# Rows of 448 bytes in place of 392 in a graph network's second layer, copied out of PSUM by one engine alone

## The reference, cut to what matters

```
def _L1_gnn_ref(features, weight, bias, src, dst, n_nodes):
    deg_out = jnp.maximum(segment_sum(ones_e, src), 1.0)
    deg_in = jnp.maximum(segment_sum(ones_e, dst), 1.0)
    h = features * (deg_out ** (-0.5))[:, None] @ weight
    rst = segment_sum(h[src], dst, num_segments=n_nodes)
    rst = rst * (deg_in ** (-0.5))[:, None] + bias
    return rst
```

## Time and profile before

| | |
|---|---|
| time, median of 3 runs | 9343.21 us (9327.21 to 9349.43) |
| span of the profiled execution | 9400.3 us |
| PE busy | 6254.5 us, 67% of the span |
| DVE busy | 5857.2 us, 62% |
| POOL busy | 5072.2 us, 54% |
| ACT busy | 2528.5 us, 27% |
| DMA queue of SP (q1) | 840.20 MB, 39.7% of 16 engines |
| DMA queue of POOL (q0) | 415.20 MB, 17.5% of 16 engines |

### The profile page before, as it was taken

How to read it: one execution, slowest core, us unless ns; L and a number is a source line. 1 busy time by engine, 2 the same in 40 slices (tenths; PEclk the granted TensorE clock), 3 DMA queues, 4 the chain that set the end, 5 groups by cost and what they waited for, 6 DMA issues and landing times. The chain is left out here.

```text
span 9400.3 us, 184649 instructions
## 1 busy us (share of the span) xinstructions
PE 6254.5 (67%) x34870; PEld 5019.0 (53%) x34871; DVE 5857.2 (62%) x19098; ACT 2528.5 (27%) x8033; POOL 5072.2 (54%) x4975
## 2 busy tenths in 40 slices
PE   1677777777756745546664455566648888888886
PEld 1566666666645533335554222555536666666664
DVE  7566666666649865558887888555554444444444
ACT  5344544545431132211110222000011222212222
POOL 0366666666657400027773000788727777777773
PEclk9555555555555655558886555787775555555556
DMA  7644444444436579998876999545743333333334
GB/s 125 142 138 136 138 138 137 137 139 139 136 95 138 119 126 187 191 190 227 228 222 123 234 252 249 147 140 145 132 102 79 80 82 80 81 80 82 79 82 32
DMA packets 1820627, 1294.74 MB, mean 138 GB/s; under 512 B 1262518, under 2 KB 1641558, under 8 KB 1818560
## 3 DMA queue, kind: packets, MB, share of 16 engines
q1 hardware_dynamic: 1578096, 840.20, 39.7%
q0 software_dynamic: 200704, 415.20, 17.5%
q10 hardware_dynamic: 40912, 29.67, 1.7%
HBM read 922.86 MB, written 361.78 MB: 137 GB/s over the span
## 5 line engine op out<-in xcount | busy, mean ns | idle before, releaser
L1095 POOL DMA_INDIRECT sorted_edges<-arena,idx x1664 | 1623.0, 975 | 951.9 <-issue 632.3
L1894 POOL DMA_INDIRECT arena<-expanded,idx x1152 | 1412.4, 1226 | 1300.8 <-DVE idx L1750 820.4
L2019 POOL DMA_INDIRECT arena<-node_table,idx x1760 | 1660.7, 944 | 557.8 <-issue 389.8
L1010 PE MATMUL banks<-arena,onehot 128*128 x3520 | 1173.1, 441 | 527.3 <-DVE onehot L946 510.6
L1010 PEld LDWEIGHTS banks<-arena,onehot 128*128 128x128 f32 x3520 | 900.6, 318 | 661.8 <-issue 615.4
L1995 PE MATMUL banks<-arena 128*128 128x64 f32 x3520 | 1215.1, 449 | 0.0
L1597 PE MATMUL banks<-arena 128*128 x3520 | 671.0, 361 | 677.2 <-issue 340.5
L1990 PE MATMUL banks<-arena 128*64 128x65 f32 x3520 | 843.7, 343 | 402.3 <-ACT arena L2006 401.4
L1995 PEld LDWEIGHTS banks<-arena 128*128 128x128 f32 x3520 | 884.5, 312 | 211.3
L1836 PE MATMUL banks<-arena 128*128 128x193 bf16 (+1 forms) x4608 | 614.3, 303 | 504.6 <-DVE arena L1802 349.9
L1965 DVE TENSOR_TENSOR arena<-arena,banks 128x64 f32 x1760 | 388.1, 221 | 876.1 <-PE banks L1995 853.8
(11 more groups left out here) (411 smaller groups left out, 11039.8 us busy)
## 6 DMA issues: line engine op xcount, KB each, us to landing
arena<-sorted_edges SPq DMA_DIRECT2D x220, 524.0 KB
arena<-lanes_dram SPq DMA_DIRECT2D x222, 512.0 KB, 13.0
expanded<-arena SPq DMA_DIRECT2D x110, 784.0 KB, 12.8
arena<-in_attr_rows SPq DMA_DIRECT2D x576, 130.0 KB
arena<-sorted_edges SPq DMA_DIRECT2D x110, 536.0 KB
arena<-row_keys SPq DMA_DIRECT2D x110, 512.0 KB
arena<-sorted_edges SPq DMA_DIRECT2D x110, 512.0 KB, 5.7
expanded<-arena SPq DMA_DIRECT2D x110, 512.0 KB
```

The costliest lines, as they stand in the source:

```text
L1010: nc.tensor.matmul(m.psum[j % 4][:, 0:D], m.onehot[:, j % 4, :], m.support[:, bass.ds(blocks[j] * D, D)], start=True, stop=True).then_inc( ...
L1095: nc.gpsimd.indirect_dma_start(m.sorted, bass.IndirectOffsetOnAxis(ap=m.idx[:, j % (4 * CH):j % (4 * CH) + 1], axis=0), m.out_ring[:, slot ...
L1894: nc.gpsimd.indirect_dma_start(to, None, rows, bass.IndirectOffsetOnAxis(ap=m.idx[:, c % aims * groups + g:c % aims * groups + g + 1], axis=0)
L2019: nc.gpsimd.indirect_dma_start(slots[:, j % SLOTS, 0:D], None, m.table, bass.IndirectOffsetOnAxis(ap=m.idx[:, j % SLOTS:j % SLOTS + 1], ax ...
```

## The change

It has three parts, and some tables move.

- `ROW2` goes from 98 to 112 words: a row is 448 bytes, seven times 64, and starts on a border of 64 bytes. The features, the count and the target number stay where they were in the row; the rest is set to zero once. A store grows from 802,816 to 917,504 bytes, a fetch of four rows in the sum by target from 1568 to 1792 bytes a partition.
- ACT copies all four groups out of PSUM. The two semaphores `put_act` and `put_dve` become one, `put`; DVE keeps `take`, and ACT waits for it before it copies groups 1 and 3.
- `reach` compares bf16 numbers (`iota16`) in place of f32.
- `onehot`, `junk`, `marks`, `below` and one of the two attribute one-hots move to another SBUF tensor; their shapes stay.

```
-ROW2 = PARTS // 2 + 2
+ROW2 = 112
+COUNT2 = PARTS // 2
+DST2 = COUNT2 + 1
...
-                    sp.wait_ge(s["put_act"], n * 2 + 2 + 2)
-                    sp.wait_ge(s["put_dve"], n * 2 + 2 + 2)
+                    sp.wait_ge(s["put"], n * 4 + 4 + 4)
...
+                v.memset(out16[:, :, :, PARTS + 4:2 * ROW2].rearrange("p c t f -> p (c t) f"), 0.0).then_inc(s["blank"], 1)
...
-                    v.tensor_scalar(m.reached[0:BUCKETS, c % 2, e, :], m.iota_row[0:BUCKETS, :], m.group_ends[0:BUCKETS, bass.ds(n * SET + e, 1)],
+                    v.tensor_scalar(m.reached[0:BUCKETS, c % 2, e, :], m.iota16[0:BUCKETS, :], m.group_ends[0:BUCKETS, bass.ds(n * SET + e, 1)],
...
-            def put(i, c, u):
-                n = i * chunks + c
-                dve.wait_ge(s["expanded"], n * 4 + u + 1 + 2 * 4)
-                to = rows_of(out16, c, u)[:, :, :, 0:PARTS]
-                v.tensor_copy(to, quad[:, 2 * u:2 * u + 2, 0:2 * PARTS].rearrange("p k (t f) -> p k t f", f=PARTS)).then_inc(s["put_dve"], 1)
-                take(i, c, u)
...
-                        elif u % 2:
-                            pe.wait_ge(s["put_dve"], n * 2 + u // 2 + 1)
-                            pe.wait_ge(s["taken"], n * 2 + u // 2 + 1)
                         else:
-                            pe.wait_ge(s["put_act"], n * 2 + u // 2 + 1)
+                            pe.wait_ge(s["put"], k + 1)
+                            if u % 2:
+                                pe.wait_ge(s["taken"], n * 2 + u // 2 + 1)
...
-                        elif u % 2 == 0:
+                        else:
                             act.wait_ge(s["expanded"], n * 4 + u + 1 + 2 * 4)
+                            if u % 2:
+                                act.wait_ge(s["taken"], n * 2 + u // 2 + 1 + 2)
```

More of the change, by code:

```diff
@@ L90 @@
 ARENA = 31104
+SCRATCH = 4 * P + 2 * P + 2 * SPARE + 4 * SPARE
 WEIGHTS = ("hamilton", "l1", "l2a", "l2b", "l3_h", "l3_b", "l3_x", "l3_agg", "l3_out")
@@ L165, in allocate @@
     at += SB * P
+    assert ROW2 * 5 * SB <= 10 * SB * D and DST2 < ROW2
     m.row_out = arena[:, at:at + 5 * SB * ROW2].rearrange("p (c t f) -> p c t f", c=5, f=ROW2)
@@ L182, in allocate @@
     at += SB * P
-    attr_onehot = arena[:, at:at + CB * P // 2]
-    assert at + CB * P // 2 <= ARENA
+    assert at <= ARENA
     at = NB * PARTS
@@ L203, in allocate @@
     m.counted = (m.ext[:, 0:2 * GP * RW], m.ext[:, 2 * GP * RW:4 * GP * RW])
-    tables = sb("edge_tables", [P, 4 * TP])
+    tables = sb("edge_tables", [P, 4 * TP + SCRATCH])
     m.ew, m.bucket = tables[:, 0:TP], tables[:, TP:2 * TP]
@@ L226, in allocate @@
     assert AIMED * 3 <= TD
-    m.onehot_attr = [part.bitcast(BF16).rearrange("p (f s) -> p f s", s=CB) for part in (attr_onehot, tables[:, free:free + CB * P // 2])]
+    m.onehot_attr = [part.bitcast(BF16).rearrange("p (f s) -> p f s", s=CB) for part in (tables[:, 4 * TP:4 * TP + CB * P // 2], tables[:, free:free + CB * P // 2])]
     m.attr_parts = [tables[:, TSX + n * PARTS:TSX + (n + 1) * PARTS] for n in range(2)]
@@ L246, in allocate @@
     m.counters = sb("counters", [P, BUCKETS])
-    m.onehot = sb("onehot", [P, 4, P])
-    m.junk = sb("junk", [P, 2, P])
+    at = 4 * TP
+    m.onehot = tables[:, at:at + 4 * P].rearrange("p (a f) -> p a f", f=P)
+    at += 4 * P
+    m.junk = tables[:, at:at + 2 * P].rearrange("p (a f) -> p a f", f=P)
+    at += 2 * P
+    m.marks = tables[:, at:at + 2 * SPARE].bitcast(BF16).rearrange("p (a f) -> p a f", f=SPARE)
+    at += 2 * SPARE
+    m.below = tables[:, at:at + 4 * SPARE].bitcast(BF16).rearrange("p (a f) -> p a f", f=SPARE)
+    assert at + 4 * SPARE == 4 * TP + SCRATCH
     m.gram = sb("gram", [D, RW])
@@ L261, in allocate @@
     m.lane_no = sb("lane_no", [P, 1])
-    m.marks = sb("marks", [P, 4, SPARE], BF16)
-    m.below = sb("below", [P, 8, SPARE], BF16)
     m.ones = sb("ones", [P, P])
@@ L1427, in expand_by_source @@
     with ExitStack() as ctx:
-        s = sems(nc, "blank", "turned", "expanded", "put_act", "put_dve", "dst", "summed", "added", "row", "reached", "found", "taken", "zeros")
+        s = sems(nc, "blank", "turned", "expanded", "put", "dst", "summed", "added", "row", "reached", "found", "taken", "zeros")
         lanes_in = ring(nc, "lanes_in", 5)
@@ L1501, in _ @@
                 v.memset(out16[:, :, :, PARTS:PARTS + 2].rearrange("p c t f -> p (c t) f"), 1.0).then_inc(s["blank"], 1)
-                dve.wait_ge(s["blank"], 1)
+                v.memset(out16[:, :, :, PARTS + 4:2 * ROW2].rearrange("p c t f -> p (c t) f"), 0.0).then_inc(s["blank"], 1)
             v.sem_inc(s["expanded"], 2 * 4)
-            v.sem_inc(s["put_dve"], 2)
             v.sem_inc(s["taken"], 2)
@@ L1525, in take @@
                 n = i * chunks + c
+                dve.wait_ge(s["expanded"], n * 4 + u + 1 + 2 * 4)
                 v.tensor_reduce(m.found[:, bass.ds(n * SET + u // 2 * (SET // 2), SET // 2)],
@@ L1557, in body @@
                         reach(i, c)
-                    if not first or c >= 5:
+                    if layer == 3 and (not first or c >= 5):
                         dve.wait_ge(stored[c % 5], i * (chunks // 5 * 16) + c // 5 * 16)
@@ L1563, in body @@
                         elif u % 2:
-                            put(i, c, u)
+                            take(i, c, u)
             body(0, True)
@@ L1624, in body @@
                             a.activation(rows, rows, ACT.Relu).then_inc(s["row"], 1)
-                        elif u % 2 == 0:
+                        else:
                             act.wait_ge(s["expanded"], n * 4 + u + 1 + 2 * 4)
+                            if u % 2:
+                                act.wait_ge(s["taken"], n * 2 + u // 2 + 1 + 2)
                             a.activation(rows_of(out16, c, u)[:, :, :, 0:PARTS],
                                          quad[:, 2 * u:2 * u + 2, 0:2 * PARTS].rearrange("p k (t f) -> p k t f", f=PARTS),
-                                         ACT.Copy).then_inc(s["put_act"], 1)
-            act.sem_inc(s["put_act"], 2)
+                                         ACT.Copy).then_inc(s["put"], 1)
+            if layer == 2:
+                act.wait_ge(s["blank"], 2)
+                act.sem_inc(s["put"], 4)
             body(0, True)
@@ L1643, in body @@
                         settle(pool)
-                        nc.gpsimd.tensor_copy(m.row_out[:, c % 5, :, ROW2 - 1:ROW2],
+                        nc.gpsimd.tensor_copy(m.row_out[:, c % 5, :, DST2:DST2 + 1],
                                               m.dst_sorted[:, bass.ds((i * chunks + c) * SB, SB)].unsqueeze(2)).then_inc(s["dst"], 1)
@@ L1790, in _ @@
                         v.tensor_tensor(lanes.rearrange("p (g t) -> p g t", t=GRAN),
-                                        m.ring2[:, c % deep, :, ROW2 - 1].rearrange("p (g t) -> p g t", t=GRAN),
+                                        m.ring2[:, c % deep, :, DST2].rearrange("p (g t) -> p g t", t=GRAN),
                                         m.block_at[:, bass.ds(n * groups, groups)].unsqueeze(2).to_broadcast([P, groups, GRAN]),
```

## The result

The changed kernel takes 9365.73 us (median of 7 runs, 9359.47 to 9378.06), the kernel before, on the same chip, 9335.21 us (9323.42 to 9349.43): ratio on record 1.0029, interval 1.0020 to 1.0039 (the two medians alone give 1.0033). It is slower, by 30 us in the medians, where 16 us less were forecast. The time lies inside the range, on the other side of no change. The profiled execution of the changed kernel took 9378.06 us, 12 us above its median.

What follows compares the result with a forecast made beforehand. Transfers were taken to pace the second layer's expansion, DVE and load latency the sum by target. Expansion -24, its end -13, fetches +21 make -16 us: 9343 - 16 = 9327 us, range 9240 to 9400.

Steps and rivals of the forecast that it cites:

- Border and store: Second-layer expansion: on 64-byte borders a store runs at 265 GB/s, 3.46 us in place of 5.5.
- the drain at the end: End of the expansion: one store left instead of five piled up, 7 us in place of 20, a gain of 13.
- Rival C: Border doesn't help, stores drain as slowly: 9454 us by bytes, 9364 by rows, middle 9409; chance 0.22.
- What takes over: Second-layer expansion: TensorE's chain, its register load held up by a freely draining store, sets 6.6 us a chunk, gaining 24 us.
- the term 1.0: Extra us a chunk for TensorE's register load held up behind a store; bounds 0.44 to 1.27.
- Rival B: Register loads aren't held up or TensorE slips past the stores: 6.0 us a chunk, 9261 us; chance 0.28.
- The sequencer's steps: TensorE in the expansion: two more steps ahead of two groups, at 46 ns, add 0.18 us a chunk.
- The comparisons: DVE in the expansion: TensorE's 111.1 us of waits for them go, but were the lateness of lanes; no gain counted.
- The base: Expansion gain reckoned from the profiled 6.82 us a chunk; that execution's 57.1 us above the timed median carried over.
- The fetches: Sum by target: 14.3% more bytes lengthen DVE's 150.1 us wait for attributes, costing 21 us; floor nothing, ceiling 63.

Runs made afterwards that it cites:

- e0b_control: The kernel before, unedited, profiled once more: one run, 9349.5 us, second-layer expansion 744.0 us, 6.76 us a chunk.
- e8_two_loads_ahead: The changed kernel with both register loads of 8 row numbers issued at the chunk's head in layer 2: ratio 0.9914 to the kernel before.
- e5_two_counters: The changed kernel with ACT's copies counted by two semaphores, so TensorE's stream is that of before: ratio 1.0011 to the kernel before.
- e1_rows_only: The kernel before with only the 448-byte rows and their zeros; copies and comparisons as before: ratio 1.0025 to the kernel before.
- the two controls: Two further profiled executions of the kernel before, unedited: 9318.6 and 9349.5 us.
- e0_control: The kernel before, unedited, profiled beside its timed runs: ratio 1.000, profiled execution 9318.6 us, expansion 708.1 us, 6.44 us a chunk.

## Why the prediction was wrong

- **Border and store: right.** The store runs flat at 300 GB/s, SP's queue doesn't fill, the drain at the end falls to some 6 us (forecast 7). Rival C is out; that its 9364, for a drain that goes by rows, lies beside the measured 9366 is chance. The rule of the Trainium skill that was set beside it (DMA: Bandwidth & Descriptors, Specifications: 512 bytes at least for the full rate, below it the engine reads, modifies and writes) doesn't fit these writes: in the slices above rows of 448 and 416 bytes ran at 230 to 360 GB/s for the most part, rows of 392 at 53 to 190.
- **What takes over: right, its cause half right.** The held-up load makes the chain the bound, as the text said. Its extra is 1.16 us (1.75 less 0.59), the term 1.0 was within its bounds. But a store needn't drain at the full rate to its end to hold a load up: those of 392 bytes in e0b_control do it too. What frees the loads is the backlog, and the change takes the backlog away. Rival B is out for this kernel; e8_two_loads_ahead, where no load is held up, comes out as it described, 5.78 us a chunk and 9246 us.
- **The sequencer's steps: the mis-sized term, and a step that failed.** "Two more sequencer steps ahead of two groups, at 46 ns" were taken as 0.18 us; they cost 0.40 (first chunk, and e5_two_counters). That is 24 us. The row of 46 ns is the length of a step's own record; between two groups the register step and the wait delay the matmuls behind them by more, 0.2 us together.
- **The comparisons: too low.** They were costed at nothing, their wait as the shadow of late lanes. The lighter VectorE gives back 0.19 us a chunk as soon as the steps are gone; in the changed kernel the steps hide it: in the chunk shown first the small matmuls start 1.42 us behind the large ones, as in e1_rows_only.
- **The base: the other failed step.** The gain was taken from 6.82 us a chunk, and the 57 us by which that execution was long were carried over "as it is". They were partly in this very stage: the two controls make 6.44 and 6.76. Against 6.59, the forecast chunk, these are between a loss of 17 us and a gain of 19 in place of the gain of 24; against the measured 6.95 they are a loss of 21 to 57.
- **The fetches: right, a little too large.** Forecast 21 us. First to last fetch is 931.8 to 947.1 us in the eight profiles with 448 bytes (mean 939.2) and 917.2 to 924.7 in the four of 392 taken beside them (mean 921.5): 18 us by these, 14 with the long execution of before; 416 bytes take 924.4. The mechanism holds too: VectorE's wait for the attributes over the whole stage is 132 to 142 us in those four (mean 138) and 144 to 168 in the eight (mean 153). The 150.1 of the earlier trace rows, in the long execution, already had part of that growth. POOL's queue went from 47.0% to 49.5% in the same window, less than the 53.7% reckoned.

Queue and wait after (DMA view, 4200 to 5140 us; VectorE's waits, 4141 to 5120 us):

```profile
q0 software_dynamic: 34466, 123.51, 49.5%
...
q1 hardware_dynamic: 78624, 72.72, 26.5%
```

```profile
DVE edge_tables L1766 <- DMA arena<-in_attr_rows: 148.1, 135, 4.8
```

What stays open: why one execution of the kernel before falls into a backlog and another doesn't, how often each kind occurs (three executions were profiled), and what inside the chip makes a register load from SBUF wait behind a store that starts at once.

## What to carry to other kernels

Where two limits lie within a few per cent of each other, lifting one gives little, and what is added to the other's chain is paid: here a register step and a semaphore wait between two groups of matmuls, together 0.2 us each time. Before a gain is reckoned from a stage of one profiled execution that is longer than the timed runs, find out whether the surplus lies in that stage. And small register loads belong ahead of a large store in time, not behind it: here moving them took the changed kernel from 1.0029 to 0.9914, and only then did the wider rows pay.

## What had not been expected of the hardware

- A register load of 8 numbers by TensorE takes 0.59 us, and 1.75 us when it comes 1.5 to 1.9 us behind the issue of a store that starts at once, with rows of 448 bytes (after) as of 392 (e0b_control). 16 numbers take 1.10 us in one load, and 2.13 us beside the third layer's stores.
- Where stores have piled up, the loads are held up less: behind the same 392-byte rows with a backlog they took 0.63 us in the median (e0_control). The kernel before so had two ways of running, 6.44 and 6.76 us a chunk in the mean of the stage.
- Rows of 416 bytes on 32-byte borders write as fast as 448 on 64-byte ones; 392 on 8-byte borders start at 250 to 280 GB/s and then fall to 80 to 165.
